# A message-passing and attention kernel: order of the first keys and checks, and begin and tail of the attention

## The reference, cut to what matters

```python
deg_isqrt = maximum(segment_sum(1, dst), 1) ** -0.5
h = maximum(layernorm(x), 0)
for W_r, W_sl, W_el in two_layers:
    self_msg = where(no_edge_into_node, h @ W_el, h @ W_sl)
    agg = segment_sum((rel_embed[rel] + h[src]) @ W_r, dst)
    h = rrelu(agg * deg_isqrt + self_msg)
x = x + h
h = maximum(layernorm(x), 0)
qk = h @ Wqk + bqk; v = h @ Wv + bv
e = exp(clip(sum(qk[dst] * qk[src]) / sqrt(128), -5, 5) - max)
out = segment_sum(e / segment_sum(e)[dst] * v[src], dst) @ Wo + bo
x = x + gamma * layernorm(out + h) + beta
```

## Time and profile before

| | us |
|---|---|
| median of 3 runs | 794.05 |
| lowest and highest | 791.5, 797.88 |
| profiled execution, its own time | 796.59 |
| span of the profile | 794.8 |
| PE busy, share of the span | 721.5, 91% |
| DVE busy | 515.8, 65% |
| ACT busy | 429.9, 54% |
| POOL busy | 239.2, 30% |
| mean granted TensorE clock | 0.924 |

### The profile page before, as it was taken

How to read it: one execution, slowest core, us unless ns; L and a number is a source line. 1 busy time by engine, 2 the same in 40 slices (tenths; PEclk the granted TensorE clock), 3 DMA queues, 4 the chain that set the end, 5 groups by cost and what they waited for, 6 DMA issues and landing times.

```text
span 794.8 us, 15460 instructions
## 1 busy us (share of the span) xinstructions
PE 721.5 (91%) x5799; PEld 537.4 (68%) x5799; DVE 515.8 (65%) x932; ACT 429.9 (54%) x1085; POOL 239.2 (30%) x272
## 2 busy tenths in 40 slices
PE   3566699989899999999999999899999999999995
PEld 2545588879789999888998999444444444444465
DVE  5798999968679777742334333444665757566667
ACT  0557556746566666662112221477676767677671
POOL 6300000000000222200000000266675767666663
PEclk7555579989999999999999999999999999999997
DMA  4102000032310000011232111210000000000000
GB/s 131 46 8 60 17 1 9 7 105 75 95 52 9 8 9 7 10 64 52 72 98 70 39 33 38 96 37 1 1 19 8 13 14 13 13 14 13 4 23 20
DMA packets 39763, 27.89 MB, mean 35 GB/s; under 512 B 5311, under 2 KB 38163, under 8 KB 39686
## 3 DMA queue, kind: packets, MB, share of 16 engines
q1 hardware_dynamic: 38514, 25.89, 11.2%
q10 hardware_dynamic: 1172, 0.98, 0.4%
HBM read 13.28 MB, written 10.80 MB: 30 GB/s over the span
## 4 chain that ended last, share of the span: by engine, by line
PE 73%; DVE 8%; issue 7%; ACT 6%; DMA 2%; SPq 2%; ACTq 1%; POOL 0%; POOLq 0%; DVEq 0%
PE sums L1503 16%; PE sums L1486 15%; PE sums L1091 12%; PE sums L1018 12%; PE sums L1057 8%; DVE work L847 2%; ACT counts L1278 2%; SPq L557 2%; DVE work L841 2%; DMA counts<-in_x 1%; PE sums L1114 1%; PE sums L1025 1%; PE sums L1098 1%; ACTq L1248 1%; PE sums L1032 1%
## 5 line engine op out<-in xcount | busy, mean ns | idle before, releaser
L1582 POOL TENSOR_TENSOR counts<-counts,work 125x500 f32<-125x500 f32 x150 | 165.3, 1102 | 95.6 <-DVE work L1643 88.5
L1057 PE MATMUL sums<-work 125*128 125x196 f16 (+15 forms) x1220 | 156.5, 255 | 19.9 <-DVE work L847 19.8
L1643 DVE SCALAR_TENSOR_TENSOR work<-sums,counts 125x500 f32<-125x500 f32 x150 | 101.7, 678 | 105.5 <-ACT sums L1600 105.5
L1503 PE MATMUL sums<-work 125*128 125x500 f32 (+1 forms) x350 | 159.0, 544 | 7.5 <-DVE work L1643 3.0
L1486 PE MATMUL sums<-work 128*125 128x500 f32 x300 | 150.5, 583 | 0.0
L1595 ACT ACTIVATE sums<-sums,work 125x500 f32<-125x500 f32 (+1 forms) x157 | 102.0, 650 | 75.3 <-PE sums L1486 72.0
L841 DVE TENSOR_TENSOR work<-work,counts 125x3024 f16<-125x3024 f16 (+1 forms) x60 | 114.2, 1904 | 40.5 <-PE sums L1059 36.9
L1059 PE MATMUL sums<-work 125*128 125x10 f16 (+15 forms) x800 | 132.9, 195 | 0.0
L1278 ACT CAST counts<-sums 128x364 f32 (+38 forms) x305 | 131.4, 472 | 2.2 <-issue 0.6
L847 DVE TENSOR_TENSOR work<-work,counts 125x4200 f16<-125x4200 f16 (+15 forms) x120 | 125.4, 1084 | 0.0
L1018 PE MATMUL sums<-counts 125*128 125x250 f16 (+1 forms) x975 | 121.7, 269 | 4.0 <-ACT work L1208 3.8
(11 more groups left out here) (177 smaller groups left out, 685.6 us busy)
## 6 DMA issues: line engine op xcount, KB each, us to landing
first_columns<-counts SPq DMA_DIRECT2D x5, 610.4 KB
counts<-first_columns SPq DMA_DIRECT2D x5, 610.4 KB
counts<-counts SPq DMA_DIRECT2D x5, 468.8 KB
counts<-in_x SPq DMA_DIRECT2D x5, 312.5 KB
h_nodes<-counts SPq DMA_DIRECT2D x5, 312.5 KB
work<-in_x SPq DMA_DIRECT2D x12, 125.0 KB
x_after_messages<-work SPq DMA_DIRECT2D x12, 125.0 KB
h_attention<-work SPq DMA_DIRECT2D x12, 125.0 KB
```

The lines of the kernel that those rows point to most:

```text
L1057: pe.matmul(win[:, 0:c, cols], lo[:, k * 2 * LO:k * 2 * LO + 128], m[:, k, h0 * w:(h0 + c) * w].rearrange("p (h d) -> p h d", d=w), start= ...
L1503: last = pe.matmul(ps_o[c % 2][:, 0:cols(u) // n], h3[:, source(c, j + i), :], pbuf[u % PB][:, i * NP:i * NP + cols(u) // n], start=j + i ...
L1582: pool.tensor_tensor(a, a, p, ALU.add).then_inc(acc_done, 1)
L1643: dve.scalar_tensor_tensor(pbuf[u % PB], ps_s[u % 4][0:NP, 0:WIDE], float(np.exp(-CLIP)), counts[0:NP, source(c, j), target(c) * WIDE:(tar ...
```

## The change

- The first keys are made in the order 0, 2, 1, 3, and ACT makes all four first copies. Ahead of them it copies one number (`woken`), which places its function table load at the start. POOL makes the table `room` later.
- `statistics` stand behind batch 2, `checks` stay behind batch 1, the flag is taken behind batch 6, `RESTS` come one batch later.
- Last chunk of layer 2: its sums release the reload of h3 in three steps; the reload is cut 2, 5, 5, 8, 4, 1 blocks; it has its own buffer (`tmp_last`) and its own PSUM columns; the aggregate product comes before the self product.
- Attention, begin: ACT's and DVE's work on units 0 and 1 is put in front of and between the last chunk's steps; `last_turn` moves from unit 1 to 3, `last_qk` from 3 to 5.
- Attention, tail: `before` of a row chunk moves into that chunk's own units 16 to 24, `ending`'s parts have other units, `before` of the last chunk comes at its third unit, most parts of `ending` of chunk 5 come behind the last weighting, and POOL does the last two parts of half 1.

In the pieces of order below the tiles `counts` and `work` are the two large SBUF tensors, `sums` is PSUM, and the brackets name semaphores. DVE at the start, before: the key copies L777, batch 0 (L841, L847), the statistics (L782 to L788), batch 1.

The diff's core (left out: POOL's move of `room`, the semaphore and buffer declarations, the new reload pieces' table, which the list above gives, and the same edits of DVE to the last chunk's buffer names):

```diff
@@ -342,7 +345,7 @@
     ROUNDS = ((22, 27, 32, 37, 42), (30, 35, 40, 45, 50))
-    RESTS = ((7, 8, 10, 11, 12), (9, 10, 12, 13, 14))
+    RESTS = ((8, 9, 11, 12, 13), (10, 11, 13, 14, 15))
@@ -611,6 +618,10 @@
             sp.dma_start(x_last, by_block(x, LAST)).then_inc(L["last_in"], 16)
+            def h3_load(i):
+                j0, j1 = T["h3_pieces"][i]
+                sp.dma_start(T["h3"][:, j0 * D:j1 * D], h3[:, j0 * D:j1 * D]).then_inc(T["h3_in"][i], 16)
             for i, c in enumerate(ORDER2[:-1]):
@@ -619,18 +630,23 @@
                     sp.dma_start(counts[0:NP, v, 0:HEAD], heads.rearrange("p (j d) -> p j d", d=HEAD)[:, v, :]).then_inc(heads_in, 16)
+                if i == LAST - 1:
+                    sp.wait_ge(L["summed"], CHUNKS)
+                    h3_load(0)
                 sp.wait_ge(L["x2_ready"], i + 1)
                 sp.dma_start(by_block(x2, c), tmp).then_inc(L["x2_out"], 16)
+                if i == LAST - 1:
+                    sp.wait_ge(L["summed"], CHUNKS + 1)
+                    h3_load(1)
                 sp.wait_ge(L["h3_ready"], i + 1)
                 sp.dma_start(h3[:, c * LB * D:(c + 1) * LB * D], xc.rearrange("p b f -> p (b f)")).then_inc(L["h3_out"], 16)
-            sp.wait_ge(L["summed"], CHUNKS)
-            sp.wait_ge(L["h3_out"], 16 * (LAST - 2))
-            for i, (j0, j1) in enumerate(T["h3_pieces"]):
-                if j0 == 0:
-                    sp.wait_ge(L["h3_out"], 16 * LAST)
-                if j0 == LAST * LB:
-                    sp.wait_ge(L["h3_last"], 16)
-                sp.dma_start(T["h3"][:, j0 * D:j1 * D], h3[:, j0 * D:j1 * D]).then_inc(T["h3_in"][i], 16)
+            sp.wait_ge(L["summed"], CHUNKS + 2)
+            for i in (2, 3):
+                h3_load(i)
+            sp.wait_ge(L["h3_out"], 16 * LAST)
+            h3_load(4)
+            sp.wait_ge(L["h3_last"], 16)
+            h3_load(5)
             sp.wait_ge(L["x2_out"], 16 * LAST)
@@ -729,13 +745,13 @@
             dve.scalar_tensor_tensor(key16[0], hi, float(-NP), src_i, ALU.mult, ALU.add).then_inc(nat_done, 1)
+            dve.wait_ge(edges_in[2], 16)
+            link(dve.tensor_scalar(rh, rel_i, float(RL), None, ALU.is_ge))
+            dve.scalar_tensor_tensor(key16[2], rh, float(-RL), rel_i, ALU.mult, ALU.add).then_inc(nat_done, 1)
             dve.wait_ge(tables_done, 2)
...
             last.then_inc(nat_done, 1)
-            dve.wait_ge(edges_in[2], 16)
-            link(dve.tensor_scalar(rh, rel_i, float(RL), None, ALU.is_ge))
-            dve.scalar_tensor_tensor(key16[2], rh, float(-RL), rel_i, ALU.mult, ALU.add).then_inc(nat_done, 1)
             for h in range(2):
@@ -772,9 +788,6 @@
             dve.scalar_tensor_tensor(words, after, 4096.0, gb, ALU.mult, ALU.add).then_inc(words_done, 1)
-            for k in (0, 2):
-                dve.wait_ge(keys_turned, k + 1)
-                dve.tensor_copy(*key_copy(k, 0)).then_inc(first_keys, 1)
@@ -853,15 +866,16 @@
                     ending(q)
-                if b == 0:
-                    statistics()
                 if b == 1:
                     checks()
+                if b == 2:
+                    statistics()
                 if b == 11:
...
                     dve.scalar_tensor_tensor(shift_x, mv[:, :, 0], -1.0, rstd, ALU.mult, ALU.mult).then_inc(scales_done, 1)
+                if b == 6:
                     dve.wait_ge(outside_sum, 1)
@@ -1108,13 +1125,20 @@
                 pe.wait_ge(L["turned_out"], i + 1)
-                if i:
+                if i == LAST:
+                    pe.wait_ge(L["summed_out"], CHUNKS)
+                    pe.wait_ge(L["x2_ready"], LAST)
+                    pe.matmul(agg_v[:, 0, :], agg_t2[:, 0:NP], wr, start=True, stop=True).then_inc(L["agg"], 1)
+                elif i:
                     pe.wait_ge(L["chunk"], i)
+                self_v = self_of(c)
                 for b in range(blocks_of(c)):
...
                     pe.wait_ge(L["wts"], 16 * 3)
+                if i == LAST:
+                    return
                 pe.wait_ge(L["summed_out"], i + 1)
@@ -1152,7 +1176,13 @@
                     own(i, c).then_inc(L["turned"], 1)
-                    sums(i, c, 0, NB)
+                    if i == LAST:
+                        for j0, j1 in ((0, 4), (4, 18)):
+                            sums(i, c, j0, j1).then_inc(L["summed"], 1)
+                        sums(i, c, 18, NB)
+                    else:
+                        sums(i, c, 0, NB)
                 else:
@@ -1181,12 +1211,14 @@
             act.dma_start(src_i, src.rearrange("(p c) -> p c", p=ROWS)).then_inc(edges_in[1], 16)
+            act.wait_ge(zeros_set, 1)
+            act.copy(woken, zeros[0:1, 0:1]).then_inc(first_keys, 1)
+            for i, k in enumerate(KEY_ORDER):
+                act.wait_ge(keys_turned, i + 1)
+                act.copy(*key_copy(k, 0)).then_inc(first_keys, 1)
             act.wait_ge(words_done, 1)
             act.dma_start(places, words).then_inc(words_in, 16)
-            for k in (1, 3):
-                act.wait_ge(keys_turned, k + 1)
-                act.copy(*key_copy(k, 0)).then_inc(first_keys, 1)
             for k in range(4):
@@ -1338,19 +1370,21 @@
                 act.copy(h_t2[:, 0:w], ps_h[:, 0:w]).then_inc(L["turned_out"], 1)
-                act.wait_ge(L["summed"], i + 1)
+                act.wait_ge(L["summed"], i + 1 if i < LAST else CHUNKS + 2)
                 act.copy(agg_t2[:, 0:w], ps_g[:, 0:w]).then_inc(L["summed_out"], 1)
+                if i == LAST:
+                    A["scalar_first"](act, 0)
                 if i:
...
                     k = c * LB + b
-                    act.mul(tmp[:, b, :], self_v[:, b, 1, :], iso[:, k:k + 1]).then_inc(L["el"], 1)
+                    act.mul(tmp_of(c)[:, b, :], self_of(c)[:, b, 1, :], iso[:, k:k + 1]).then_inc(L["el"], 1)
                 if i:
                     rows(i - 1, ORDER2[i - 1])
-            A["scalar_first"](act)
+            A["scalar_first"](act, 1)
             act.wait_ge(L["x2_ready"], CHUNKS)
-            act.dma_start(by_block(x2, LAST), tmp[:, 0:1, :]).then_inc(L["x2_last"], 16)
+            act.dma_start(by_block(x2, LAST), tmp_last).then_inc(L["x2_last"], 16)
@@ -1441,12 +1476,13 @@
     N_AT, F_AT, BEGIN_AT = 3, 4, 6
-    BEFORE_AT = ((3, 4, 5), (10, 11, 15))
-    ENDING_AT = ((7, 8, 9, 12, 13, 14), (16, 17, 18, 21, 22, 23))
-    ROOT_AT = (10, 19)
+    BEFORE_AT = ((16, 20, 21), (22, 23, 24))
+    ENDING_AT = ((7, 8, 9, 11, 12, 13), (10, 14, 15, 17, 18, 19))
+    ROOT_AT = (9, 15)
     LAST_N, LAST_F = 0, 1
-    LAST_ENDING = ((), (), ((0, 0), (0, 1)), ((0, 2), (1, 0), (1, 1)), ((1, 2), (0, 3)), ((0, 4), (0, 5), (1, 3)), ((1, 4), (1, 5)))
+    LAST_ENDING = ((), (), ((0, 0),), ((0, 1),), ((0, 2),), ((1, 0),), ((1, 1), (1, 2), (0, 3), (0, 4), (0, 5), (1, 3)))
@@ -1527,16 +1563,16 @@
         for u, (c, j, n) in enumerate(units):
-            if u + AHEAD < len(units):
+            if u and u + AHEAD < len(units):
                 score(pe, u + AHEAD)
...
             weighted(u)
-            if u == 1:
+            if u == 3:
                 last_turn()
-            if u == 3:
+            if u == 5:
                 last_qk()
@@ -1584,8 +1620,14 @@
                         root(c - 1, h, m)
-            if c == FULL and j in (3 * AB, 4 * AB):
-                root(FULL - 1, j // AB - 3, 2)
+            if c == FULL and j in (4 * AB, 6 * AB):
+                root(FULL - 1, j // AB // 2 - 2, 2)
+        v = y[1]
+        pool.wait_ge(var_done[1], FULL + 1)
+        pool.tensor_tensor(v, v, gamma_b[:, None, :].broadcast_to([NP, 2, D]), ALU.mult).then_inc(zero_set, 1)
+        pool.wait_ge(zero_set, 3)
+        pool.tensor_tensor(v, v, xr[1], ALU.add).then_inc(y_ready[1], 1)
         root(FULL, 0, 1)
@@ -1616,11 +1658,11 @@
                 below(act, u + 1)
-            if u:
+            if u > 1:
                 exponent(act, u)
-            if u == 1:
+            if u == 3:
                 last_turned()
-            if u == 3:
+            if u == 5:
                 last_rows()
@@ -1725,32 +1774,31 @@
         for u, (c, j, n) in enumerate(units):
-            if u:
+            if u > 1:
                 weigh(dve, u)
...
                 dve.tensor_copy(bv_w, bv_c.broadcast_to([D, NP])).then_inc(bvb, 1)
+            if c < FULL:
+                for h, m in halves(c):
+                    if c == 0 and h == 0 and j == BEFORE_AT[0][1]:
+                        dve.wait_ge(wvo_out, 2)
+                    if j in BEFORE_AT[h]:
+                        before(c, h, m, BEFORE_AT[h].index(j))
             if 0 < c < FULL:
                 for h, m in halves(c - 1):
-                    if c == 1 and h == 0 and j == BEFORE_AT[0][0]:
-                        dve.wait_ge(wvo_out, 2)
-                    if j in BEFORE_AT[h]:
-                        before(c - 1, h, m, BEFORE_AT[h].index(j))
                     if j == BEGIN_AT and h == 0:
...
                 k = j // AB
```

(7 more changed lines are left out.)

72 lines of the change are left out of this document (44 added, 28 removed).

## The result

| | before | after |
|---|---|---|
| median of 20 runs each, us | 794.4 | 790.74 |
| lowest and highest | 791.5, 798.8 | 785.36, 795.61 |
| profiled execution, its own time | 796.59 | 794.31 |
| span of the profile | 794.8 | 792.6 |
| mean granted TensorE clock | 0.924 | 0.983 |

The ratio after to before is 0.9965, with an interval of 0.9948 to 0.9982: 0.35% faster, 2.8 us (the two medians alone differ by 3.7). Gains in us that stand beside a ratio are taken from the ratio. Forecast were 783.0 us and a gain of 10.8; the time lies just outside the range of 777 to 790. Most single steps came out as worked out, and two waits that the prediction had costed at nothing took most of it back. The mean clock is no effect of the change: executions of before have about 0.93 in some cases and 0.99 in others. One of the 12 executions of experiment 2 took 3991.55 us and is not in its ratio.

What follows compares the result with a forecast made beforehand. DVE was taken to set the pace in the first 100 us, PE inside the attention. Gains 7.0 + 1.3 + 0 + 2.5 = 10.8 off 796.59 gave 785.8, or 783.0 against the median; range 777 to 790.

Steps and rivals of the forecast that it cites:

- Front, 7.0: First 100 us: earlier keys, statistics behind batch 2 and later `RESTS` gain 7.0 us, bounds 4 and 8.
- The two mechanisms: Start: new key order starts batch 0 4.2 us earlier; statistics behind batch 2 remove DVE's 2.43 us wait for x.
- `RESTS`, 0: Message layers, 60 to 80 us: rests one batch later remove DVE's 2.0 us wait for h's stores; no separate gain.
- Passage, 1.3: Message layers to attention: earlier h3 reload gains 1.62 us, waits at units 4 and 6 cost 0.3; bounds 0 and 3.
- Middle, 0: Inside the attention: `before` moves to its own chunk's units 16 to 24; 0, with 1 us either way.
- Tail, 2.5: Last 20 us: less DVE work between weightings, two parts on POOL; gain 2.5 us, bounds 0.5 and 3.8.
- Half of the front: Rival: late relation ids or POOL's root leave the front 4, passage 0, tail 1: 789 us; chance 0.17.
- The slower case: Rival: more ACT stalls in 155 to 225 us, three costing 18, give 801 us; chance 0.05.
- The base: Profiled execution 796.59 less 10.8 gives 785.8; it lies 2.5 above the median 794.05, so 783.2, said as 783.0.

Runs made afterwards that it cites:

- experiment 2: The changed kernel with `RESTS` as before, one batch earlier: 789.66 us, ratio 0.9931 to the kernel before.
- experiment 9: The kernel before with only the front of the change, without the `RESTS` shift: 786.43 us, ratio 0.992.
- experiment 4: The changed kernel, SP waiting for the last x2 store to land before issuing the third and fourth reload of h3: 785.64 us, ratio 0.9896.
- experiment 7: Changed kernel with last chunk's x2 in free columns, `RESTS` as before, and half 1's last two parts back on DVE: 782.16 us, ratio 0.987.
- experiment 3: The changed kernel with the last chunk's x2 in free columns of its own and `RESTS` as before: 782.29 us, ratio 0.9855 to the kernel before.

## Why the prediction was wrong

By its steps, the traces' numbers behind each:

- *Front, 7.0.* The two mechanisms are right: without `RESTS`, 6.05 at batch 12 and 6.3 in the times (experiment 9). Batch 0 was forecast at 17.5 to 17.9 and came at 18.15, since DVE still waits 0.90 for POOL's table; relation ids were in time. POOL's root cost 0.19. That the keys need the statistics' move (3.7 with it, nothing that shows without) is in the numbers of the earlier trace rows, where x lands at 27.18, and the prediction did not draw it.
- *`RESTS`, 0: this step failed.* The prediction said that one batch later "takes that wait away, but there ACT, not DVE, is in front". The wait for h's stores went, as said. But ACT, in front, came for a rest (L886) 5.0 us before it was there, because that rest now had batch 11 and the relations ahead of it. It cost 1.9 us in the trace and 2.4 in the times (0.9885 to 0.9855, whose intervals overlap; 0.9965 to 0.9931 says 2.7). Its own sentence, that ACT is in front, was the argument against: a step that an engine in front waits for may not be moved back.
- *Passage, 1.3: right but for one thing that was costed at nothing, and this is the main failure.* From the sums to the first weighting the gain is 1.57 (forecast 1.62); the waits at units 4 and 6 are 1.52 and 1.44 (forecast 1.7 each; by its own numbers, 3.4 against 3.0, the passage should have been 1.2 and not 1.3). With the buffer elsewhere the passage gives 1.57 + 0.10 = 1.7. The step that failed is "Chunk 12 in its own buffer and bank no longer waits for the store of x2; that wait was hidden". The buffer lies under the fourth unit's weights, and the wait stands in DVE's row at that unit; the store is issued at about the first weighting, with two large pieces of the reload ahead of it, and landed 8.58 us later (at most 2.1 with these held back, experiment 4). This cost 7.6 us in the trace and 6.4 in the times.
- *Middle, 0.* Exactly that: 249.71 us from the eighth weighting to the last row chunk's first, in before and in after.
- *Tail, 2.5.* It gave 3.4. The last weighting came 3.8 earlier within its row chunk (forecast 3.3 to 4.0); DVE's work behind it took 2.95 us (783.81 to 786.76) and not 3.4 to 4.2, since POOL's root beside it (784.98) slowed nothing: L1764 took 0.59 for two beside the root and again behind it, and L1771 0.43, the length that it has with POOL idle (experiment 7). The Trainium skill, page SBUF — State Buffer, section "SBUF: two separate sides", has a DVE operation with two SBUF inputs and one of POOL exclude each other for a whole instruction; by it the tail was to give 1.2. The trace does not test that on POOL's two parts: they ended at 788.36, and DVE's next operation with two SBUF inputs came at 789.33. With them on DVE the tail is 0.8 longer, so by the traces handing them over paid; the times do not tell the two apart. Where POOL was in its product of 500 columns, DVE's L1760 took 0.94 and ended at 782.51, 0.03 behind POOL, and 0.35 at 784.56, ending again 0.03 behind it; on one column and with no such product beside it the line took 0.15. That looks like the exclusion, the rows beside the root do not, and so the rule alone does not price a change.
- *The rivals.* None had this mechanism. "Half of the front" gave the nearest time, 789, for another reason. The slower case, stalls that come and go, does exist, but it shows between executions of one program, and not as an effect of the change.
- *The base.* 785.8 was taken 2.5 down to the median. The second execution of before took 797.13 us, again above every median of before; why is open, and the ratios do not need it.

The parts add up: front 6.3 and tail 3.3 as measured each alone, and passage 1.7 by the trace, give 11.3, and experiment 3 measured 11.5. Each of the three measured gains carries an interval of some 2 us either way. Of the 8.7 us between experiment 3 and the change as it is, the store's wait took 6.4 and `RESTS` 2.4.

## What to carry to other kernels

A buffer that is placed over another's memory brings a wait at that other's first use: look for the wait in the rows of the instruction that writes there, and price it by when the transfer can land behind what is queued ahead of it, not by its own size. When a load is issued earlier, list the small transfers that are issued behind it and who waits for them. A step of DVE may be moved back without cost only if the engine that takes its result is not in front; and two edits that each shorten the way to one late transfer must be priced together.

## What had not been expected of the hardware

A store of one block took 8.58 us from issue to landing behind four pieces of reload, 20 blocks, on another engine's queue, and at most 2.1 with the two large ones, 13 blocks, held back. The first 60 us took the same at either level of TensorE's clock: the granted clock was 1.00 there in after and 0.57 in experiment 3, and batch 3 started at 38.89 and 38.95. DVE sets the pace there, as the earlier trace rows said, and PE's speed bought nothing. And one program differed by 4 us between two executions in one stretch (360.2 and 356.3 of after): a span's difference of a few us between two profiles says little before it is cut into stretches.
